# Two layers of adaptive-norm attention and feed-forward: the second layer's modulation and attention weights prepared inside the first feed-forward stage

## The reference

```python
mod = (silu(c) @ wmod).reshape(8, 6, 1, 128)          # wmod: 128 x 768
sa, ca, ga, sb, cb, gb = (mod[:, k] for k in range(6))
ga = (2 * (ga >= 0) - 1) * maximum(abs(ga), 0.25)      # the same for gb
x = x + ga * attention(layernorm(x) * (1 + ca) + sa)
x = x + gb * ffn(layernorm(x) * (1 + cb) + sb)
```

## Time and profile before

| | |
|---|---|
| time, median of 3 runs | 1547.29 us (1547.27 to 1548.33) |
| the profiled execution | 1553.07 us |
| its span, first to last instruction | 1551.1 us |
| mean granted clock of PE | 0.862 of full |
| `f0` with its weights | about 877 to 1094 us of the span |
| `modulation` of layer 1 | 1094.56 to 1121 |
| `layer1_weights` | 1121.7 to 1138.7 |
| attention of layer 1 | 1138.8 to 1343 |
| `f1` with its weights | 1343 to 1542 |

### The profile page before, as it was taken

How to read it: one execution, slowest core, us unless ns; L and a number is a source line. 1 busy time by engine, 2 the same in 40 slices (tenths; PEclk the granted TensorE clock), 3 DMA queues, 4 the chain that set the end, 5 groups by cost and what they waited for, 6 DMA issues and landing times. The chain is left out here.

```text
span 1551.1 us, 29838 instructions
## 1 busy us (share of the span) xinstructions
PE 1149.9 (74%) x10864; PEld 718.6 (46%) x10864; DVE 1105.2 (71%) x1557; ACT 608.0 (39%) x1176; POOL 841.0 (54%) x772
## 2 busy tenths in 40 slices
PE   2388999989999899999999436555448886165554
PEld 1135565645655556556565424333214676133343
DVE  2377978868789588797878458986227775469983
ACT  1134545545455354564546123332124330133331
POOL 0267878869788597987979213331026564023320
PEclk9578999999999899999999858988655898668896
DMA  2221212212121121221211000000000000000001
GB/s 69 74 43 43 43 33 53 43 31 49 34 55 37 24 63 33 53 43 22 63 33 33 15 0 1 0 0 1 14 11 1 1 1 1 14 0 0 1 0 55
DMA packets 48100, 42.17 MB, mean 27 GB/s; under 512 B 7734, under 2 KB 46154, under 8 KB 47946
## 3 DMA queue, kind: packets, MB, share of 16 engines
q1 hardware_dynamic: 47946, 40.14, 11.4%
HBM read 6.42 MB, written 2.10 MB: 5 GB/s over the span
## 5 line engine op out<-in xcount | busy, mean ns | idle before, releaser
L661 POOL TENSOR_TENSOR a_p_lo<-a_probs 128x512 f16<-128x512 f32 x384 | 418.6, 1113 | 29.1 <-ACT a_probs L515 25.3
L515 ACT ACTIVATE a_probs<-a_ps_s 128x512 f32<-128x512 f32 x512 | 304.0, 597 | 327.2 <-PE a_ps_s L447 322.7
L597 DVE TENSOR_REDUCE a_nmx<-a_ps_m 128x2 f32<-128x1024 f32 x256 | 311.0, 1216 | 33.4 <-PE a_ps_m L430 32.6
L463 PE MATMUL a_ps_o<-a_v_hi,a_probs 128*128 128x65 f16 x2048 | 243.0, 196 | 7.6 <-POOL a_p_lo L661 7.6
L464 PE MATMUL a_ps_o<-a_v_lo,a_probs 128*128 128x64 f16 x2048 | 240.3, 194 | 0.0
L465 PE MATMUL a_ps_o<-a_v_hi,a_p_lo 128*128 128x65 f16 x2048 | 240.0, 194 | 0.0
L463 PEld LDWEIGHTS a_ps_o<-a_v_hi,a_probs 128*128 128x128 bf16 x2048 | 189.3, 98 | 79.1 <-issue 48.5
L445 PE MATMUL a_ps_s<-a_qq,a_kk 128*128 128x512 f16 x512 | 198.0, 387 | 10.4 <-issue 6.2
L464 PEld LDWEIGHTS a_ps_o<-a_v_lo,a_probs 128*128 128x128 bf16 x2048 | 191.1, 99 | 25.1 <-issue 1.0
L447 PE MATMUL a_ps_s<-a_qq,a_k_l 65*128 65x512 f16 x512 | 198.6, 388 | 0.0
L465 PEld LDWEIGHTS a_ps_o<-a_v_hi,a_p_lo 128*128 128x128 f16 x2048 | 190.9, 98 | 0.0
(11 more groups left out here) (218 smaller groups left out, 2105.9 us busy)
## 6 DMA issues: line engine op xcount, KB each, us to landing
a_qq<-a_rhi SPq DMA_DIRECT2D x128, 128.0 KB, 2.4
a_qq<-a_rlo SPq DMA_DIRECT2D x128, 64.0 KB, 2.1
a_kk<-a_rhi SPq DMA_DIRECT2D x64, 64.0 KB, 2.0
a_k_l<-a_rlo SPq DMA_DIRECT2D x32, 64.0 KB, 2.0
out_x<-x_sb SPq DMA_DIRECT2D x1, 2048.0 KB, 8.7
a_qq<-a_nmT SPq DMA_DIRECT2D x64, 2.0 KB
m_w<-in_wmod SPq DMA_DIRECT2D x2, 384.0 KB
a_probs<-in_wq SPq DMA_DIRECT2D x1, 512.0 KB, 3.7
```

The lines of the kernel that those rows point to most:

```text
L463: nc.tensor.matmul(out, hi, v_hi[:, b % 2, kt, g, 0:65], start=(kt == 0), stop=False)
L515: nc.scalar.activation(probs[:, p % 2, kt, h, :], ps_s[:, i % 2, :], ACT.Exp, scale=DH0 ** -0.5).then_inc(exp_done, 1)
L597: nc.vector.tensor_reduce(nmx[:, p % 2, i:2 * QT:QT], ps_m[:, n % 2, :, :], axis=X, op=ALU.max, negate=True).then_inc(free[n % 2], 1)
L661: nc.gpsimd.tensor_tensor(p_lo[:, p % 2, kt, h, :], pr, pr.bitcast(BF16)[:, 1:2 * L:2], ALU.subtract).then_inc(lo_pool, 1)
```

## The change

`ffn` gets an argument `nxt`; for "f0" it carries the inputs of layer 1 and the tensors that the attention of layer 1 needs. The blocks of `modulation` for layer 1 and of `layer1_weights` are gone; their work is spread over the steps of `f0`. `mod_bc1` is a tensor of its own, since `mod_bc` is still in use.

- SP issues 16 loads at the start of the stage and three small DMAs when their sources are ready.
- PE does 13 pieces, named in `prepared`, at three places of a step: B (behind `gate_up(i, 1)`), C (ahead of the transposes into `ps_h`) and A (at the end). All of them write `ps_h`; each waits until ACT has read the one before (`p_read`), and the transposes wait for the pieces numbered ahead of them.
- ACT copies each piece out at the same place of its own list, makes `gm`, scales q's bias and makes the high fp16 halves.
- DVE does the two small reductions at i = 0 and, at i = 2, adds 1 and clamps the gates on `m8`, the modulation with one sequence on each of 8 partitions. For each sequence one matmul against `chosen` (the row of the unit matrix repeated 128 times) then spreads its row of `m8` over all partitions.
- POOL makes silu(c) and `chosen` at i = -1, five of the 15 copies of `bias` at each of i = 0, 1, 2, small products and differences at i = 3 and 4, and `wo_g` at i = 6, each behind the step's own work.

```diff
+            prepared = {(0, "A"): ("cT",), (1, "B"): ("modT",), (1, "C"): ("m8",), (1, "A"): ("qkv",),
+                        (2, "B"): ("gates",), (2, "A"): ("bc", 0)}
+            for b in range(1, B):
+                prepared[3 + (b - 1) // 3, "BCA"[(b - 1) % 3]] = ("bc", b)
...
+                for dst, src in loads:
+                    sp.dma_start(dst, src).then_inc(n_loaded, 16)
+                sp.wait_ge(b_lo_ok, 1)
+                sp.dma_start(b_hl[1:2, :], b_lo[:]).then_inc(moved, 16)
...
             for i in STEPS:
                 if has(i):
                     gate_up(i, 1)
+                prepare(i, "B")
                 if has(i - 1):
                     turn(i - 1, 0)
                     down(i - 1, 0)
                     turn(i - 1, 1)
                     down(i - 1, 1)
+                prepare(i, "C")
                 if has(i + 1):
+                    ahead = sum(k[0] < i or (k[0] == i and k[1] in "BC") for k in number)
+                    if ahead:
+                        pe.wait_ge(p_read, ahead)
                     pe.wait_ge(q1_ok, i + 2)
...
                     gate_up(i + 1, 0)
+                    prepare(i, "A")
```

A piece on PE and on ACT:

```diff
+                else:
+                    pe.wait_ge(m8_ok, 1)
+                    last = nc.tensor.matmul(ps_h[:], chosen[:, what[1], :], m8[:].rearrange("p k d -> p (k d)"),
+                                            start=True, stop=True)
+                last.then_inc(p_full, 1)
...
+                else:
+                    b = what[1]
+                    nc.scalar.activation(mod_bc1[:, b, :, :].rearrange("p k d -> p (k d)"), ps_h[:], ACT.Copy
+                                         ).then_inc(p_read, 1)
+                    if b == 4:
+                        act.wait_ge(b_ok, 1)
+                        nc.scalar.activation(b_hl[0:1, :], b_all[:], ACT.Copy).then_inc(b_hi_ok, 1)
+                        act.wait_ge(bo_g_ok, 1)
+                        nc.scalar.activation(bo_hi8[:], bo_g[:], ACT.Copy).then_inc(bo_hi_ok, 1)
...
+                if nxt is not None and i == -1:
+                    act.wait_ge(n_loaded, LOADS * 16)
+                    nc.scalar.activation(sg[:], c_n[:], ACT.Sigmoid).then_inc(sg_ok, 1)
```

DVE and POOL:

```diff
+                if nxt is not None and i == 2:
+                    gates = m8[:, 0:4:3, :]
+                    dve.wait_ge(m8_raw, 1)
+                    nc.vector.tensor_scalar(m8[:, 2, :], m8[:, 2, :], 1.0, None, ALU.add)
+                    nc.vector.tensor_scalar(sgn[:], gates, 0.0, 2.0, ALU.is_ge, ALU.mult)
+                    nc.vector.tensor_scalar(mag[:].bitcast(I32), gates.bitcast(I32), 0x7FFFFFFF, None,
+                                            ALU.bitwise_and)
+                    nc.vector.drain()
+                    nc.vector.tensor_scalar(mag[:], mag[:], 0.25, None, ALU.max)
+                    nc.vector.drain()
+                    nc.vector.scalar_tensor_tensor(out=gates, in0=sgn[:], scalar=-1.0, in1=mag[:], op0=ALU.add,
+                                                   op1=ALU.mult).then_inc(m8_ok, 1)
...
+                if 0 <= i < 3:
+                    flat = bias[:].rearrange("p t s h -> p (t s) h")
+                    for rel in range(1 - B + 5 * i, 6 - B + 5 * i):
...
+                if i == 6:
+                    pool.wait_ge(p_read, len(number))
+                    nc.gpsimd.tensor_tensor(wo_g[:], wo_t[:].unsqueeze(1).to_broadcast([D, B, D]),
+                                            mod_bc1[:, :, 0, :], ALU.mult)
```

In `program`:

```diff
-        ffn(nc, x_sb, mod_bc, ident, dict(w_gate=t["wg0"], w_up=t["wu0"], w_down=t["wd0"]), "f0")
-        modulation(nc, ex, sb, t["c1"], t["wmod1"], modT, mod_bc, ident, "m1")
...
+        ffn(nc, x_sb, mod_bc, ident, dict(w_gate=t["wg0"], w_up=t["wu0"], w_down=t["wd0"]), "f0",
+            (dram1, modT, mod_bc1, w_all, b_hl, wo_g, bo_hl, bias, grep_a))
+        layer1_attention(nc, x_sb, modT, ident, w_all, b_hl, wo_g, bo_hl, bias, grep_a)
+        ffn(nc, x_sb, mod_bc1, ident, dict(w_gate=t["wg1"], w_up=t["wu1"], w_down=t["wd1"]), "f1")
```

More of the change, by code:

```diff
@@ L31 @@
 NR = 4
+H1, DH1 = 16, 8
+NBUCK = 32
+NG = 2 * H1
+NW = 3 * D + NG
+HB = B // 2
 def modulation(nc, ctx, sb, c, wmod, out_t, out_bc, ident, tag):
@@ L812, in ffn @@
         STEPS = range(-2, B + 1)
+        if nxt is not None:
+            dram1, modT, mod_bc1, w_all, b_hl, wo_g, bo_hl, bias, grep_a = nxt
+            c_n, sg, s_n, bo8, bo_g = (sb(n, [B, D]) for n in ("c_n", "sg", "s_n", "bo8", "bo_g"))
+            bo_hi8, bo_lo8 = sb("bo_hi8", [B, D], FP16), sb("bo_lo8", [B, D], FP16)
+            cT, wmod, m8 = sb("cT", [D, B]), sb("wmod", [D, 6 * D]), sb("m8", [B, 4, D])
+            sgn, mag, chosen = sb("sgn", [B, 2, D]), sb("mag", [B, 2, D]), sb("chosen", [B, B, 128])
+            w4, wo_t = sb("w4", [D, 4, D]), sb("wo_t", [D, D])
+            gw, gws, gm, mask = sb("gw", [D, 8]), sb("gws", [D, 2]), sb("gm", [D, NG]), sb("mask", [D, H1])
+            bq, one = sb("bq", [D, 1]), sb("one", [D, 1])
+            gb, gbs, pg_row = sb("gb", [1, 8]), sb("gbs", [1, 2]), sb("pg_row", [1, NG])
+            b_all, b_lo = sb("b_all", [1, NW]), sb("b_lo", [1, NW], FP16)
+            table = sb("table", [128, NBUCK, H1])
+            (n_loaded, sg_ok, silu_ok, cT_ok, gws_ok, gm_ok, m8_raw, m8_ok, bc_ok, wo_t_ok, b_ok, b_hi_ok, b_lo_ok,
+             bo_g_ok, bo_hi_ok, bo_lo_ok, p_full, p_read, moved, one_ok) = (
+                sem(n) for n in ("nld sg silu cT gws gm m8r m8 bc wot b bhi blo bog bohi bolo pf pr moved one").split())
+            q_scale = DH1 ** -0.5
+            LOADS = 16
+            prepared = {(0, "A"): ("cT",), (1, "B"): ("modT",), (1, "C"): ("m8",), (1, "A"): ("qkv",),
+                        (2, "B"): ("gates",), (2, "A"): ("bc", 0)}
+            for b in range(1, B):
+                prepared[3 + (b - 1) // 3, "BCA"[(b - 1) % 3]] = ("bc", b)
+            number = {}
+            for i in STEPS:
+                for place in "BCA":
+                    if (i, place) in prepared:
+                        number[i, place] = len(number)
+        else:
+            prepared, number = {}, {}
@@ L1119, in layer1_attention @@
-def layer1_attention(nc, x_sb, modT, mod_bc, ident, dram):
+                if nxt is None:
+                    continue
+                if i == -1:
+                    pool.wait_ge(sg_ok, 1)
+                    nc.gpsimd.tensor_tensor(s_n[:], c_n[:], sg[:], ALU.mult).then_inc(silu_ok, 1)
+                    nc.gpsimd.memset(one[:], 1.0).then_inc(one_ok, 1)
+                    nc.gpsimd.drain()
+                    nc.gpsimd.tensor_copy(chosen[:], ident[0:B, 0:B].unsqueeze(2).to_broadcast([B, B, 128]))
@@ L1121, in layer1_attention @@
+def layer1_attention(nc, x_sb, modT, ident, w_all, b_hl, wo_g, bo_hl, bias, grep_a):
     tag = "a1"
```

220 lines of the change are left out of this document (110 added, 110 removed).

## The result

The changed kernel takes 1520.87 us in the median of four runs (1519.29 to 1521.89), the kernel before 1547.28 (1546.82 to 1548.33): a ratio of 0.9827, 95% interval 0.981 to 0.9844. That is 26.4 us or 1.7% faster. The forecast was 1509.8 us with a range of 1502 to 1519: the direction came true, the gain is 11.1 us smaller than forecast, and the time lies 1.9 us outside the range. The profiled execution of after took 1520.90 us, its span is 1518.8.

A forecast was written before the change was run, and what follows sets the result against it. DVE was taken to bound each step of `f0`. Removing 44.2 + 1.3 us and adding 8.0 gave 37.5 us off the 1547.29 median: 1509.8 us, range 1502 to 1519.

The forecast's parts named there:

- Removed: Behind `f0`, the modulation and layer 1 weight blocks go: 44.2 us saved, plus 1.3 for a table load.
- The table load of 1.3 us: At the attention's first sigmoid, ACT no longer needs to load a table: 1.3 us saved, counted in full.
- DVE, 1.9: In `f0` at i = 0 and 2, added reductions, gate instructions and drains cost 1.9 us (1.3 to 4).
- POOL, 4.8 together: In `f0`, POOL's added work takes turns with DVE: copies 3.4 us, small products 1.0, `wo_g` 0.4.
- PE and ACT, 1.9: In `f0`, pieces and their copies delay `c2`, so DVE stalls: 0.4 and 1.5 us (0 to 3.5 together).
- At i = 1 (`m8`) and 2 (`gates`) the stalls above cover it: 0: In steps 1 and 2, DVE's stalls under POOL hide the pieces' delay: 0 us, or 1.2 without them.
- the terms of i = 3 and 4: In steps 3 and 4, DVE stalls for late `c2` 1.35 and 2.1 us; less POOL's stalls, 0.4 and 1.5.
- The clock credit, 0.6: In `f0`, PE idles less and half-clock `gate_up(i,1)` gains, shortening DVE's waits: 0.6 us credited (0 to 3.7).
- rival (a): The preparation fits into `f0`'s slack: `f0` changes by -1.8 to +3.5 us, 1500 to 1505.3; chance 18%.
- Rival (b): The added work on all engines shows in full in `f0`: 13 to 20 us, 1515 to 1522; chance 15%.
- Rival (c): No gain or slower: `f0` becomes PE-bound at 1.2 GHz throughout, 44 us over eight steps; chance 2%.
- The signs that I named: Attention 0.3 us behind `f0`, no table load, L938 or L940 longer, L927 waiting at i = 3 and 4, i = 5 and 7 unchanged.

The follow-up runs named there:

- e12: e2's kernel once more, unedited, to see whether its longer attention repeats: 1508.7 us, attention again 189.2.
- e6: e5 with GpSimd's bias copies and small products moved between `q1` and the layer norm; all work kept: 1508.0 us, ratio 0.9746.
- e13: e2's kernel with only GpSimd's first five bias copies put back, ahead of `q2` in step 0: 1512.8 us; step 1 24.70 us.
- e3: The change with its 13 pieces and ACT's copies, but without VectorE's and GpSimd's work for them and SP's three moves: 1513.0 us, ratio 0.9769.
- e5: The change with all 13 pieces moved to the ends of steps, GpSimd's rest halves and `wo_g` one step later: 1512.65 us, ratio 0.9777.
- e8: The change plus one unread 128x512 matmul ahead of the down products in steps 1 and 4: 1516.2 us, ratio 0.9805.
- e14: e13's kernel plus one unread 128x512 matmul on PE ahead of step 1's down products: 1508.0 us; step 1 22.06 us.
- e2: The change without the preparation work, keeping the loads, `silu` and `chosen`; the attention reads zeros: 1509.9 us, ratio 0.9766.
- e10: e6's kernel plus five unread matmuls on PE at the start of the second attention: 1508.3 us, ratio 0.974.
- e15: The change with no piece at place C, pieces at B and A instead, GpSimd's rest halves and `wo_g` one step later: 1515.8 us, ratio 0.9796.
- e9: e6's kernel plus five unread 128x512 matmuls on PE in the last turn of each feed-forward: 1506.5 us, ratio 0.9732.

## Why the prediction was wrong, step by step

**Removed: nearly right.** Forecast 44.2 for the gap, measured 42.1 between representative profiles. Of the difference 1.7 us are the longer wait for a load in the first profile. That its execution was 5.8 us off the median was there to be seen (1553.07 against 1547.29), and I took a stretch of loads and barriers from it as if only DVE and ACT set its length. The table load of 1.3 us is gone, and the attention's first `prob` product did come 1.1 us earlier after the start (51.8 instead of 52.9). Even that is not surely the table's: among the kernels without this load the moment lies between 48.4 and 51.8 us, with PE's clock. And it wasn't banked: the attention as a whole is 0.4 longer, `f1` 1.8. That these 3.5 us (1.3 + 0.4 + 1.8) come from PE's clock is likely by e12 but not shown. For `f1` the change may be no part of it: the unchanged kernel's two profiles have 198.1 and 196.0, the change 197.8. The 11.1 us between forecast and result are so 2.1 from the gap, 3.5 from the stages behind it and 6.1 from `f0`, less 0.7 in the stages' small differences.

**DVE, 1.9: close.** The block of step 2 took 2.4 us, one of its instructions 1.14 instead of some 0.3 because it ran beside POOL's `q1`:

```profile
969.67 0.27 DVE L1101 TENSOR_SCALAR f_sgn<-f_m 8x256 f32<-8x256 f32 x1
969.87 1.14 DVE L1102 TENSOR_SCALAR f_mag<-f_m 8x256 int32<-8x256 int32 x1
971.09 0.28 DVE L1105 TENSOR_SCALAR f_mag<-f_mag 8x256 f32<-8x256 f32 x1
```

**POOL, 4.8 together: the mechanism right, its direct price too high.** The copies took 4.3 us on POOL, as forecast. L938 (now L1080) was held 2.19 us in step 1 (1.37 in e6, which has no copies there) and 1.96 in step 3 (1.54), which is 1.2 us of turns and not 3.4. In steps 4 and 5, where DVE had waited and `q2` was through, the same instruction took 0.69 instead of 1.54, and 1.7 us came back. `wo_g` held DVE's small L1057, 1.77 instead of 0.21. The indirect price is the one that I didn't have: up to the 3.5 us of e13.

```profile
936.71 2.19 DVE L1080 TENSOR_TENSOR f_h<-f_xhat,mod_bc 128x512 f32<-128x512 f32 x1 [1.17 <-ACT f_xhat L1041]
...
984.13 1.96 DVE L1080 TENSOR_TENSOR f_h<-f_xhat,mod_bc 128x512 f32<-128x512 f32 x1
```

**PE and ACT, 1.9: the step that failed.** Two sentences were wrong. "At i = 1 (`m8`) and 2 (`gates`) the stalls above cover it: 0": the stall of DVE for `c2` in step 1 is 3.50 us. And the terms of i = 3 and 4, 1.35 and 2.1 before cover, were worked out with durations at full clock: in step 3, where the down products ran at full clock, the wait is 1.22, right; in step 4 it is 4.22, twice the forecast. The terms were sums of the pieces' own lengths; what they left out is that all of PE's other work in the step runs at half speed when the clock doesn't come up: 2.93 instead of 1.60 for each group of down products, 4.44 instead of 2.63 for the gate and up products. The pieces without any other part cost 10.5 us (e3); in the change, 8.1 of its 14.1 us go when the same pieces stand at the ends of the turns (e5).

**The clock credit, 0.6: it came, and a cost of the same kind that I didn't have outweighed it.** I argued that PE with more work idles less and so keeps its clock. In steps 2, 3, 5 and 6 it did: DVE's waits for `sig` there fell from 3.6 to 1.8 us, and the last down products of the tail took 1.60 instead of 2.93, most of the tail's 1.5. In step 4 the same waits grew from 0.3 to 1.9. What I missed is the other direction. Work helps where it fills the idle stretch, as the filler of e8 and e14 does. 0.88 us on POOL ahead of `q2` fill nothing: they delay what ends the stretch, and the stretch grows.

The Trainium skill (TensorE: Matmul & The Clock Gate, HAM oscillation) says that idle gaps throttle PE. I had it speak for rival (a) because pieces fill gaps; e13 and e14 agree with the rule and show it cutting the other way in step 1.

**The rivals.** Rival (b), 13 to 20 us and 1515 to 1522, is the one that came in size (14.1, 1520.9), at a chance of 15%. Its reason was another: the sum of all upper bounds at full clock, with POOL's 8.6 first. Rival (c) named the right mechanism, a PE left at 1.2 GHz, but only as an all or nothing over eight steps; it happened in two, and not throughout them. The range ended at 1519 because it took in half of (b).

**The signs that I named.** The attention 0.3 us behind `f0`: 0.27, its first instruction on POOL (0.72 on DVE). No table load: right. L938 beyond 1.54 at i = 1 and 3: right; at i = 2: 1.54, wrong. L927 waiting at i = 3 and 4: right, and at i = 1 as well. Steps 5 and 7 as before: -0.8 and -1.5, shorter.

**What stays open.** Which clock pattern a kernel gets in the attention, worth up to 7.6 us between e2 (189.2) and e6 (181.6), was not set by any edit on purpose; e10 moved the clock and not the time. I can't say what decides it, nor how much of e6's margin over e5 (4.6 us in the medians; in the profiles 3.5 in `f0` and 3.3 in the attention) comes from there. Open too is what besides the idle stretch decides PE's clock in `f0`, in step 4 above all, where 1.77 us of it went with the lower level.

## What to carry to other kernels

Before adding work to a step, look at PE's idle stretches and at whether the work behind them ran at half clock: here 0.88 us on GpSimd that lengthened such a stretch cost 3.5 us, and a matmul that filled it paid 2.6 of them back. Whether it does so elsewhere has to be tried: with a piece at B in the same step (e15) the same 0.88 us cost 0.9. Put added pieces behind the step's last product that somebody waits for, not ahead of it, even where each slack by itself seems to hold them: moving the same thirteen pieces and GpSimd's copies (and its rest halves and `wo_g` a step later) made this change 12.9 us better (1520.9 to 1508.0). And take a stage's length from an execution near the median; if the profiled one is 5.8 us off, ask first in which stage.

## What the runs showed of the hardware

- A matmul that nobody reads made a step 4.0 us shorter (e8) and 2.6 (e14), by having PE at 2.4 instead of 1.2 GHz for the next 10 us. Some of it was lost again in the next two steps: `f0` as a whole was 3.8 and 3.1 us shorter.
- In step 1 PE, idle for 2.14 us, came back up within the first down products, and after 2.57 and 2.96 us it did not. The same idle length does not give the same clock elsewhere (2.20 us with the upper level in step 2 of the change, 1.77 with the lower in step 4), and the 4.19 us left behind five fillers were enough for half clock (e9).
- DVE's small tensor_scalar instructions (one SBUF operand) were held beside GpSimd too: beside `wo_g`, POOL's product of 128x1024, the 128x88 one takes 1.77 us instead of 0.21.

```profile
1065.23 2.40 POOL L1198 TENSOR_TENSOR wo_g<-f_wo_t,mod_bc 128x1024 f32<-128x1024 f32 x1
```

```profile
1065.93 1.77 DVE L1057 TENSOR_SCALAR f_s<-f_s 128x88 f32<-128x88 f32 x1
```

- Code that is the same gives stages that differ: e13 and e14 have e2's attention, and took 189.2 and 181.7 us in it. `f1` took 198.1 and 196.0 us in two executions of the unchanged kernel.
